# A transformer block on one Trainium2 core: normalising the next stage's first tile in the stage ahead, loops written out on two engines, and two fp32 matmuls split in two

## Chip, cores and metric

The kernel runs on one core of a Trainium2 chip. Its time is the device time of one execution, in microseconds (us). A core has four computing engines, each with a queue of its own: TensorE (PE in the profile), VectorE (DVE), ScalarE (ACT) and GpSimd (POOL). SyncE (SP) issues most DMAs. The engines run side by side and meet only at semaphores: an instruction that waits for one holds up everything behind it on its own engine.

## What is computed

A block of three residual steps over 8 sequences of 1024 tokens with 512 features, all in fp32: half a feed-forward, an attention with a delta rule, and half a feed-forward again.

```python
x = x + 0.5 * ffn(layernorm(x))
x = x + attn(layernorm(x))
x = x + 0.5 * ffn(layernorm(x))

# ffn: x_prev is x one token earlier, zero at a sequence's start
xr = mu_r * x + (1.0 - mu_r) * x_prev
xk = mu_k * x + (1.0 - mu_k) * x_prev
out = sigmoid(xr @ W_r.T) * (square(relu(xk @ W_k.T)) @ W_v.T)

# attn, first part (the stage "ain"): a causal convolution of 4 taps
q = silu(short_conv_1d(x @ Wq + bq, q_conv)); k, v likewise; q, k then divided by their norms per head
alpha, beta, gate = sigmoid(x @ Wa + ba), sigmoid(x @ Wb + bb), silu(x @ Wg + bg)
```

## The kernel before

Everything is stored with features on the 128 partitions and tokens along the free axis: a tile is [128, 4, 512], that is 512 features of 512 tokens. There are NT = 16 tiles. Five stages follow one another, with a barrier of all engines between them: the first feed-forward (`ffn1`), the q/k/v stage (`ain`), the recurrence (`rec`), the attention's output (`aout`) and the second feed-forward (`ffn2`). Both feed-forwards come from `ffn_phase`, the q/k/v stage from `attn_in_phase`. Each engine's program is written by hand, and its order is the order of the calls in `slot(...)`; nothing is scheduled.

**Products.** Every large product is made of three fp32r matmuls (`product`, L46): weight and operand are each split into a high and a low part of reduced precision, and high x high, high x low and low x high are added up in PSUM. A 512x512 product of a tile is 4 groups `m` of 12 matmuls.

**Layer norm.** VectorE adds the four feature tiles to one (`sums`, L178 and L180 in `ffn_phase`), TensorE multiplies by a matrix of 1/512 (`mean`, one fp32 matmul of 512 columns), VectorE subtracts (`centre`), ScalarE squares, GpSimd adds (`squares`), TensorE takes the variance per token (`var`), then VectorE adds epsilon (L200), ScalarE takes the root, VectorE the reciprocal (L202) and lays it on diagonals (L204), and TensorE spreads it over all partitions with a matrix of ones (`spread_rstd`, one fp32 matmul). VectorE multiplies (`normalise`).

**Feed-forward slots.** In slot `t` TensorE does `mean(t + 1)`, r (4 groups), k group 0, `var(t + 1)`, k group 1, `spread_rstd(t + 1)`, k groups 2 and 3, then v. The last slot, `slot(NT - 1, False)`, has no tile ahead and leaves the three small steps out. VectorE, ScalarE, GpSimd and TensorE run these slots in loops (`Fori`) with a few written out at the ends.

**The q/k/v stage.** In slot `t` TensorE does alpha/beta (12 matmuls, `ain_ps_ab`), then twelve groups u of q, k and v with four gate groups between them; `var(t + 1)` stands behind group 3, `spread_rstd(t + 1)` and `mean(t + 2)` behind group 5 and the second gate group. ScalarE reads each group out of PSUM (`shift`), VectorE convolves it (`convolve`: two copies of 3 columns and three operations of 512), ScalarE applies silu. A slot of VectorE begins with `mask_tails` (L806), which zeroes the 3 columns carried over from the tile before where a sequence starts, and ends with `decays`. SyncE stores decay rows only after `decays` (`ends_ready`): 4 DMAs, 4 more, and then the gate tile (L687); ScalarE's next gate group waits for that store. VectorE and ScalarE run two slots in one round of a `Fori` (L891 on VectorE), six rounds, slots 1 to 12; slot 0 and slots 13 to 15 are written out.

**The start of the q/k/v stage.** SyncE loads tile 0, the weight q, alpha/beta weights, 12 tiny bias pieces, weights g, k, v, biases and taps, then tile 1. VectorE goes through sums(0), casts of q and k, centre(0), the low parts, alpha/beta weights, the norm of tile 0, sums(1), the low part of tile 0, centre(1). TensorE stands at mean(0), var(0), spread_rstd(0), mean(1) and then the first slot.

## Time and profile before

| | us |
|---|---|
| median of 3 runs | 3439.56 (3439.38 to 3450.98) |
| the profiled execution: its own time | 3438.4 |
| its span, first to last instruction | 3436.7 |
| ffn1, up to its last VectorE instruction | 602.3 |
| first instruction of ain / first alpha/beta matmul | 607.2 / 643.25 |
| first matmul of ain's last slot | 1471.2 |
| TensorE busy | 3218.8 (94%) |
| VectorE busy | 2755.4 (80%) |

Times in the trace count from the span's start. A row of a timeline is an instruction, or several alike, with its start, its duration and the engine; "[2.40 <-ACT ...]" says that the engine had been idle for 2.40 us and what ended that. A matmul's duration includes filling the array, so the distance from one start to the next is what it takes of TensorE, not its duration. An fp32 matmul shows as two rows (x2). A wait "for issue" is idle time for which the profile knows no semaphore.

### The profile page before, as it was taken

The page shows a single profiled execution, that of the slowest core. Times are in us where ns is not written, and L with a number is a line of the kernel's source. Part 1 is how long each engine was busy: PE and PEld are TensorE (multiplying, and loading weights), DVE is VectorE, ACT ScalarE, POOL GpSimd, SP SyncE. Part 2 cuts the span into 40 slices and gives each one's busy share as a digit, 9 for nine tenths or more (in the row PEclk, how much of TensorE's full clock was granted, in tenths as well). Part 3 has the DMA queues.
Part 4 walks back from the last instruction along what each step waited for, and adds up shares of the span by engine and source line. Part 5 has one row for each costly group of instructions (what it writes and reads, how often), then busy time and mean ns, then how long its engine had stood idle before and what let it go on. Part 6 is the DMA issues. An engine that isn't in the chain of part 4 may idle for free. (4 is left out here: it accounts for less than half of the span.)

```text
span 3436.7 us, 190745 instructions
## 1 busy us (share of the span) xinstructions
PE 3218.8 (94%) x83236; PEld 2722.1 (79%) x83236; DVE 2755.4 (80%) x4776; ACT 1516.0 (44%) x2285; POOL 1300.2 (38%) x1195
## 2 busy tenths in 40 slices
PE   7999999699999999977999999999996988999999
PEld 5888888477777767757999999999995766888887
DVE  6776765798898989876999999999997857767765
ACT  4545454467676777751111111111113324455454
POOL 1232232200000000005788888888884421232322
PEclk9999999799999999988999999999997998999999
DMA  3112121233332323236777777777765772121221
GB/s 123 73 73 110 73 110 52 108 113 93 98 102 89 103 92 103 86 102 165 198 199 200 199 201 199 200 201 199 199 182 172 228 230 99 73 106 77 79 104 61
DMA packets 486578, 453.14 MB, mean 132 GB/s; under 512 B 55504, under 2 KB 448848, under 8 KB 467280
## 3 DMA queue, kind: packets, MB, share of 16 engines
q1 hardware_dynamic: 483632, 449.50, 43.4%
q10 hardware_dynamic: 2848, 2.56, 0.3%
q8 instruction: 35, 0.57, 0.1%
q14 instruction: 63, 0.52, 0.0%
HBM read 331.33 MB, written 120.60 MB: 132 GB/s over the span
## 5 line engine op out<-in xcount | busy, mean ns | idle before, releaser
L350 POOL TENSOR_TENSOR ffn_out<-ffn_gate,ffn_xres 128x512 f32<-128x512 f32 x128 | 171.0, 1364 | 783.6 <-DVE ffn_gate L254 783.2
L819 DVE SCALAR_TENSOR_TENSOR ain_conv<-ain_padded,ain_taps,ain_conv 128x512 f32<-128x512 f32 x576 | 447.2, 776 | 20.5
L1530 ACT ACTIVATE rec_u<-rec_ps_end 128x256 f32<-128x256 f32 x128 | 49.0, 383 | 632.2 <-PE rec_ps_end L1582 632.2
L909 POOL TENSOR_TENSOR ain_half<-ain_sq 128x1024 f32<-128x1024 f32 x16 | 44.8, 2797 | 731.9 <-ACT ain_sq L925 731.9
L1298 POOL TENSOR_TENSOR rec_d_norm<-rec_dmat,rec_early 128x512 f32<-128x512 f32 x128 | 162.7, 1271 | 176.0 <-DVE rec_dmat L1380 176.0
L46 PE MATMUL ffn_ring<-ffn_mixkh,ffn_wkh 128*128 128x512 f32 x512 | 218.2, 426 | 6.5 <-DVE ffn_mixkl L196 6.5
L46 PE MATMUL ffn_ring<-ffn_mixrh,ffn_wrh 128*128 128x512 f32 x512 | 215.2, 420 | 9.2 <-DVE ffn_mixrl L306 9.2
L46 PE MATMUL ffn_ring<-ffn_mixkh,ffn_wkl 128*128 128x512 f32 x512 | 202.8, 396 | 0.0
L46 PE MATMUL ffn_ring<-ffn_mixrh,ffn_wrl 128*128 128x512 f32 x512 | 201.7, 394 | 0.0
L46 PE MATMUL ffn_ring<-ffn_act_h,ffn_wvh 128*128 128x512 f32 x512 | 201.6, 394 | 0.0
L46 PE MATMUL ffn_ring<-ffn_mixkl,ffn_wkh 128*128 128x512 f32 x512 | 201.1, 393 | 0.0
L46 PE MATMUL ffn_ring<-ffn_act_h,ffn_wvl 128*128 128x512 f32 x512 | 200.9, 392 | 0.0
L46 PE MATMUL ffn_ring<-ffn_mixrl,ffn_wrh 128*128 128x512 f32 x512 | 200.0, 391 | 0.0
L46 PE MATMUL ffn_ring<-ffn_act_l,ffn_wvh 128*128 128x512 f32 x512 | 198.7, 388 | 0.0
L959 ACT ACTIVATE ain_buf<-ain_conv 128x512 f32<-128x512 f32 x192 | 120.9, 630 | 160.7 <-DVE ain_conv L819 159.8
L1582 PE MATMUL rec_ps_scores<-rec_qk_pe,rec_kb 32*32 32x64 f32 x8192 | 143.1, 218 | 35.8 <-POOL rec_kb L1290 29.7
L1304 POOL TENSOR_TENSOR rec_d_pair<-rec_d_norm,rec_masks 128x512 f32<-128x512 f32 x128 | 163.0, 1274 | 10.0
L1329 POOL TENSOR_TENSOR rec_gqk<-rec_qkv,rec_late 128x512 f32<-128x512 f32 x128 | 163.0, 1273 | 0.7 <-PE rec_ps_chain L1582 0.7
L200 DVE TENSOR_SCALAR ffn_var_tok<-ffn_mean 128x4 f32<-128x4 f32 x30 | 4.9, 163 | 193.8 <-PE ffn_mean L453 193.8
L1582 PE MATMUL rec_ps_chain<-rec_kwp,rec_u 32*32 32x64 f32 x8192 | 143.5, 217 | 17.4 <-issue 15.1
L374 ACT ACTIVATE ffn_mixkh<-ffn_mixk 128x2048 fp32r<-128x2048 f32 x32 | 61.4, 1919 | 213.9 <-DVE ffn_mixk L189 213.9
L1582 PEld LDWEIGHTS rec_ps_scores<-rec_qk_pe,rec_kb 32*32 32x32 f32 x8192 | 122.3, 106 | 37.5 <-issue 36.7
(247 smaller groups left out, 9888.4 us busy)
## 6 DMA issues: line engine op xcount, KB each, us to landing
rec_early<-coeffs SPq DMA_DIRECT2D x512, 128.0 KB, 3.0
streams<-ain_buf SPq DMA_DIRECT2D x48, 1024.0 KB, 5.1
rec_qkv<-streams SPq DMA_DIRECT2D x126, 384.0 KB, 3.4
rec_qk_pe<-streams SPq DMA_DIRECT2D x127, 256.0 KB, 3.3
rec_late<-coeffs SPq DMA_DIRECT2D x504, 64.0 KB, 2.3
ffn_xres<-in_x SPq DMA_DIRECT2D x16, 1024.0 KB
ain_x<-x SPq DMA_DIRECT2D x16, 1024.0 KB, 4.8
gate<-ain_gate SPq DMA_DIRECT2D x16, 1024.0 KB, 4.2
```

The source lines that it names most:

```text
L46: last = nc.tensor.matmul(out, w[:, k, m * width:(m + 1) * width], x[:, k, :], start=(k == 0 and n == 0), stop=(k == KT - 1 and n == 2))
L200: nc.vector.tensor_scalar_add(var_tok[:], ps_var[:, 0:KT], LN_EPS).then_inc(var_copied, 1)
L350: added = nc.gpsimd.tensor_tensor(out[:, m, :], gate[:, m, :], xres[:, m, :], ALU.add)
L374: nc.scalar.activation(mix_h[n][:], mix[n][:], ACT.Copy).then_inc(mix_high, 1)
L819: nc.vector.scalar_tensor_tensor(out=out[:], in0=pad[:, n:n + TOK], scalar=taps[:, u // KT, u % KT, n:n + 1], in1=out[:], op0=ALU.mult, op ...
L909: nc.gpsimd.tensor_tensor(half2[:], sq[:, 0:2, :], sq[:, 2:4, :], ALU.add).then_inc(halved2, 1)
L959: nc.scalar.activation(view, conv[u % 3][:].rearrange("p (c i) -> p c i", i=CH), ACT.Silu).then_inc(silued, 1)
L1298: nc.gpsimd.tensor_tensor(d_norm[:], dmat[:].unsqueeze(1).to_broadcast(pair), early[s][:, K_QNORM:K_KNORM + 1].rearrange("p k b g i -> p k ...
L1304: nc.gpsimd.tensor_tensor(d_pair[:], d_norm[:, 1].unsqueeze(1).to_broadcast(pair), masks[:, IN_BLOCK:OFF_BLOCK + 1, :].rearrange("p w (g i ...
L1329: nc.gpsimd.tensor_tensor(gqk[:].rearrange("p w (b g) i -> p w b (g i)", b=2), qkv[s][:, :, NQ:NK_ + 1].rearrange("p b w g i -> p w b (g i)"),
L1530: nc.scalar.activation(u[:], ps_end[:, :, 1, :], ACT.Copy).then_inc(u_ready, 1)
L1582: last = nc.tensor.matmul(out(rows, g), lhs_t(rows, g), rhs(rows, g), start=g in firsts, stop=True, skip_group_check=True)
```

## The change

1. **Tile 0 of ain is normalised in ffn1.** A buffer `normed` outlives both stages and takes the place of `xc` in both. ffn1 gets `norm_next=True`: its slot NT - 2 also loads tile 0 of its own output and sums it, and its last slot does mean, centre, squares, variance, deviation and spread for it, and then `normalise_next`. ain starts with `high(0, 0)` and `low(0, 0)`, its semaphores for the skipped steps are raised at once, and the loads and preparations are put in another order; all four high parts of the weights are ScalarE's now.
2. **VectorE's and ScalarE's ain programs are written out**, all 16 slots. `mask_tails` becomes `clear_tails`, a memset in even slots alone. TensorE, GpSimd and SyncE keep their loops.
3. **Mean and spread in both feed-forwards are split in high and low part**: two fp32r matmuls in place of one fp32 matmul each, for all means but those of tiles 0 and 1, and all spreads. ScalarE makes `sum_h`, VectorE `sum_l`; `sums(t + 2)` moves ahead of `mix_rest(t + 1, "r", 0)`. The reciprocal is split by two operations of 4 columns, and the diagonals are 1024 wide instead of 512.

```diff
@@ ffn_phase @@
+        rstd_diag = sb("rstd_diag", [P, 2, KT, P], F32R)
 ...
+            def sum_rest(t):
+                dve.wait_ge(sum_high, t - 1)
+                nc.vector.tensor_tensor(sum_l[:], sum1[:], sum_h[:].bitcast(F32), ALU.subtract).then_inc(sum_split, 1)
 ...
-                nc.vector.tensor_tensor(rstd_diag[:], ident[:].unsqueeze(1).to_broadcast([P, KT, P]),
-                                        rstd_tok[:].unsqueeze(2).to_broadcast([P, KT, P]), ALU.mult).then_inc(diagonal, 1)
+                nc.vector.tensor_copy(rstd_split[:, 0, :], rstd_tok[:]).then_inc(rstd_high, 1)
+                dve.wait_ge(rstd_high, t + 1)
+                nc.vector.tensor_tensor(rstd_split[:, 1, :], rstd_tok[:], rstd_split[:, 0, :].bitcast(F32),
+                                        ALU.subtract).then_inc(rstd_low, 1)
+                dve.wait_ge(rstd_low, t + 1)
+                nc.vector.tensor_tensor(rstd_diag[:], ident[:].unsqueeze(1).unsqueeze(1).to_broadcast([P, 2, KT, P]),
+                                        rstd_split[:].bitcast(F32).unsqueeze(3).to_broadcast([P, 2, KT, P]),
+                                        ALU.mult).then_inc(diagonal, 1)
 ...
+            def normalise_next():
+                dve.wait_ge(spread, NT + 1)
+                nc.vector.tensor_tensor(xc[:], xc[:], ps_rstd[:].unsqueeze(1).to_broadcast([P, KT, TOK]), ALU.mult)
 ...
-            slot(NT - 2, 1)
-            slot(NT - 1, 0)
+            slot(NT - 2, 2 if norm_next else 1)
+            slot(NT - 1, "norm" if norm_next else 0)
 ...
+            def sum_round(t):
+                act.wait_ge(summed, t)
+                act.wait_ge(mean_done, t)
+                nc.scalar.activation(sum_h[:], sum1[:], ACT.Copy).then_inc(sum_high, 1)
 ...
-                pe.wait_ge(summed, t)
-                nc.tensor.matmul(ps_mean[:], mean_w[:], sum1[:], start=True, stop=True).then_inc(mean_done, 1)
+                    pe.wait_ge(sum_split, t - 1)
+                    nc.tensor.matmul(ps_mean[:], mean_r[:], sum_h[:], start=True, stop=False)
+                    nc.tensor.matmul(ps_mean[:], mean_r[:], sum_l[:], start=False, stop=True).then_inc(mean_done, 1)
 ...
+                for part in range(2):
+                    last = nc.tensor.matmul(ps_rstd[:], ones_r[:], rstd_diag[:, part].rearrange("p j n -> p (j n)"),
+                                            start=(part == 0), stop=(part == 1))
 ...
@@ attn_in_phase @@
-            sp.dma_start(x[:], src[0, :, :, :]).then_inc(x_loaded, 16)
+            sp.sem_inc(x_loaded, 16)
+            sp.dma_start(wab_in[:], wab_dram).then_inc(ab_loaded, 16)
             sp.dma_start(stage["q"], w_dram["q"]).then_inc(w_loaded["q"], 16)
+            sp.wait_ge(centred, 1)
+            sp.dma_start(x[:], src[1, :, :, :]).then_inc(x_loaded, 16)
+            for n in "gkv":
+                sp.dma_start(stage[n], w_dram[n]).then_inc(w_loaded[n], 16)
 ...
-                nc.vector.tensor_tensor(tail[:].unsqueeze(1), tail[:].unsqueeze(1), start_mask[:, bass.ds(t, 1), :, :],
-                                        ALU.mult).then_inc(tails_masked, 1)
+                nc.vector.memset(tail[:], 0.0).then_inc(tails_masked, 1)
 ...
-            with dve.Fori(0, NT // 2 - 2) as r:
-                slot(2 * r + 1, 1)
-                slot(2 * r + 2, 0)
-            slot(NT - 3, 1)
+            for t in range(1, NT - 2):
+                slot(t, t % 2)
 ...
-            mean(0)
-            var(0)
-            spread_rstd(0)
+            for done in (mean_done, var_done, spread_done):
+                pe.sem_inc(done, 1)
             mean(1)
```

VectorE, late in a feed-forward slot of the loop, behind the low parts of the activation, before (`ffn_half` and `ffn_sum` are the sums of the tile after next, `mixr` and `mixk` the operands of r and k):

```order
L196 TENSOR_TENSOR ffn_mixrl<-ffn_mixr,ffn_mixrh 128x2048
L177 REGISTER_ALU
L178 TENSOR_TENSOR ffn_half<-ffn_x 128x1024
L180 TENSOR_TENSOR ffn_sum<-ffn_half 128x512
L189 SCALAR_TENSOR_TENSOR ffn_mixk<-ffn_diff,ffn_mu,ffn_xn 128x512 x4
```

The same place after the change:

```order
L189 TENSOR_TENSOR ffn_half<-ffn_x 128x1024
L191 TENSOR_TENSOR ffn_sum<-ffn_half 128x512
L210 REGISTER_ALU
L211 TENSOR_TENSOR ffn_mixrl<-ffn_mixr,ffn_mixrh 128x2048
L195 TENSOR_TENSOR ffn_sum_l<-ffn_sum,ffn_sum_h 128x512
L204 SCALAR_TENSOR_TENSOR ffn_mixk<-ffn_diff,ffn_mu,ffn_xn 128x512 x4
```

The sums moved ahead of r's low part, and one operation of 512 columns was added behind it.

VectorE at the start of ain, before, from the first operation that reads data to the second centring:

```order
L772 TENSOR_TENSOR ain_half<-ain_x 128x1024
L774 TENSOR_TENSOR ain_half<-ain_half 128x512
L722 CAST ain_wqh<-ain_buf 128x2048
L780 TENSOR_TENSOR ain_xc<-ain_x,ain_ps_mean 128x2048
L726 TENSOR_TENSOR ain_wql<-ain_buf,ain_wqh 128x2048
L722 CAST ain_wkh<-ain_buf 128x2048
...
L796 TENSOR_TENSOR ain_xc<-ain_xc,ain_ps_rstd 128x2048
L772 TENSOR_TENSOR ain_half<-ain_x 128x1024
L774 TENSOR_TENSOR ain_half<-ain_half 128x512
L801 TENSOR_TENSOR ain_xl<-ain_xc,ain_xh 128x2048
L767 TENSOR_TENSOR ain_bias_tap<-ain_bias,ain_taps 128x12
L780 TENSOR_TENSOR ain_xc<-ain_x,ain_ps_mean 128x2048
```

And after:

```order
L844 TENSOR_TENSOR ain_xl<-normed,ain_xh 128x2048
L800 COPY ain_conv<-ain_wab_in 128x16x4 x3
L804 CAST ain_wab_h<-ain_conv 128x512
L806 TENSOR_TENSOR ain_wab_l<-ain_conv,ain_wab_h 128x512
L768 TENSOR_TENSOR ain_wql<-ain_buf,ain_wqh 128x2048
L815 TENSOR_TENSOR ain_half<-ain_x 128x1024
L817 TENSOR_TENSOR ain_half<-ain_half 128x512
...
L768 TENSOR_TENSOR ain_wkl<-ain_buf,ain_wkh 128x2048
L810 TENSOR_TENSOR ain_bias_tap<-ain_bias,ain_taps 128x12
L823 TENSOR_TENSOR normed<-ain_x,ain_ps_mean 128x2048
```

The low part of tile 0 is first, the casts have left VectorE, and only one sum and one centring (of tile 1) stand ahead of slot 0.

VectorE at the end of a round of ain's loop, before (the next row is the first of the slot after the loop; inside, the branch goes back to slot 2r + 1):

```order
L830 SCALAR_TENSOR_TENSOR ain_gamma<-ain_decay,ain_alpha_beta 128x512
L832 COPY ain_gamma_end<-ain_gamma 128x16
L891 REGISTER_ALU
L891 COMPARE_AND_BRANCH
L806 TENSOR_TENSOR ain_tail<-ain_tail,ain_start_mask 128x36
L814 COPY ain_padded<-ain_tail 128x3
```

And after, between slots 0 and 1:

```order
L872 SCALAR_TENSOR_TENSOR ain_gamma<-ain_decay,ain_alpha_beta 128x512
L874 COPY ain_gamma_end<-ain_gamma 128x16
L856 COPY ain_padded<-ain_tail 128x3
L858 COPY ain_tail<-ain_padded 128x3
```

The branch is gone, and in odd slots nothing stands between the decays and the first convolution.

## Rows read from the trace of the kernel before

**Rows 1.** The page's costliest groups: ScalarE's copy of a whole tile to fp32r.
```profile
L374 ACT ACTIVATE ffn_mixkh<-ffn_mixk 128x2048 fp32r<-128x2048 f32 x32 | 61.4, 1919 | 213.9 <-DVE ffn_mixk L189 213.9
```

**Rows 2.** Busy time by stretch: span; PE, PEld, DVE, ACT, POOL; clock; DMA.
```profile
0.00:601.60 601.60, 581.79 (x2506) 465.40 (x2506) 413.81 (x458) 294.62 (x361) 157.97 (x99) 0.99 0.23 88
601.60:643.20 41.60, 8.05 (x14) 3.28 (x14) 31.86 (x39) 8.91 (x6) 17.05 (x8) 0.54 0.45 173
643.20:1471.20 828.00, 801.55 (x3478) 605.02 (x3478) 734.86 (x1131) 596.19 (x850) 62.27 (x30) 0.99 0.31 95
```

**Rows 3.** Timeline of TensorE: a mean in ffn1 and the matmuls behind it.
```profile
176.66 1.02 PE L447 MATMUL ffn_mean<-ffn_sum,ffn_mean_w 128*128 128x512 f32 x2
...
177.75 0.39 PE L46 MATMUL ffn_ring<-ffn_mixrl,ffn_wrh 128*128 128x512 f32 x1
177.97 0.39 PE L46 MATMUL ffn_ring<-ffn_mixrh,ffn_wrl 128*128 128x512 f32 x1
```

**Rows 4.** Waits in 40 to 602 us: TensorE's largest (total, times, longest).
```profile
PE ffn_ring L46 <- DVE ffn_mixkl L196: 3.3, 1, 3.3
```

**Rows 5.** Timelines of VectorE and TensorE in the same slot of ffn1.
```profile
157.28 0.69 DVE L204 TENSOR_TENSOR ffn_rstd_diag<-ffn_ident,ffn_rstd_tok 128x512 f32<-128x512 f32 x1
...
171.06 2.29 DVE L196 TENSOR_TENSOR ffn_mixrl<-ffn_mixr,ffn_mixrh 128x2048 fp32r<-128x2048 f32 x1 [0.86 <-ACT ffn_mixrh L374]
...
174.52 0.69 DVE L180 TENSOR_TENSOR ffn_sum<-ffn_half 128x512 f32<-128x512 f32 x1
...
159.31 1.02 PE L459 MATMUL ffn_rstd<-ffn_rstd_diag,ffn_ones 128*128 128x512 f32 x2
```

**Rows 6.** Timelines of SyncE, VectorE and TensorE at ain's start.
```profile
607.21 0.34 SPq L645 DMA_DIRECT2D ain_x<-x  x1
...
612.52 1.22 DVE L772 TENSOR_TENSOR ain_half<-ain_x 128x1024 f32<-128x1024 f32 x1 [2.61 <-DMA ain_x<-x]
...
641.05 2.08 PE L1055 MATMUL ain_ps_mean<-ain_half,ain_mean_w 128*128 128x512 f32 x2 [6.32 <-DVE ain_half L774]
643.25 0.79 PE L46 MATMUL ain_ps_ab<-ain_xh,ain_wab_h 128*128 128x512 f32 x1
```

**Rows 7.** DMA issues: count, KB each, median us from issue to landing.
```profile
ain_buf<-in_wq SPq DMA_DIRECT2D x1, 1024.0 KB, 7.0
...
ain_buf<-in_wv SPq DMA_DIRECT2D x1, 1024.0 KB, 10.1
```

**Rows 8.** Waits in 660 to 1500 us, within ain: total, times, longest.
```profile
ACT ain_gate L974 <- DMA gate<-ain_gate: 37.1, 10, 5.7
...
PE ain_ps_rstd L1067 <- DVE ain_rstd_diag L791: 26.3, 10, 4.0
DVE ain_tail L806 <- issue: 24.5, 6, 4.9
...
DVE ain_rstd_tok L789 <- ACT ain_std_tok L929: 21.3, 10, 2.4
```

**Rows 9.** Timeline of VectorE: the first instruction of ain's slots 2, 3, 4, 12, 13 and 14.
```profile
759.89 0.20 DVE L806 TENSOR_TENSOR ain_tail<-ain_tail,ain_start_mask 128x36 f32<-128x36 f32 x1
...
819.06 0.20 DVE L806 TENSOR_TENSOR ain_tail<-ain_tail,ain_start_mask 128x36 f32<-128x36 f32 x1 [4.79 <-issue]
...
870.97 0.20 DVE L806 TENSOR_TENSOR ain_tail<-ain_tail,ain_start_mask 128x36 f32<-128x36 f32 x1
...
1319.02 0.20 DVE L806 TENSOR_TENSOR ain_tail<-ain_tail,ain_start_mask 128x36 f32<-128x36 f32 x1
...
1374.63 0.20 DVE L806 TENSOR_TENSOR ain_tail<-ain_tail,ain_start_mask 128x36 f32<-128x36 f32 x1
...
1428.84 0.19 DVE L806 TENSOR_TENSOR ain_tail<-ain_tail,ain_start_mask 128x36 f32<-128x36 f32 x1
```

**Rows 10.** Timelines of SyncE and VectorE in ain's slot 2.
```profile
764.11 0.36 SPq L687 DMA_DIRECT2D gate<-ain_gate  x1
...
775.22 0.18 DVE L789 RECIPROCAL ain_rstd_tok<-ain_std_tok 128x4 f32<-128x4 f32 x1 [2.40 <-ACT ain_std_tok L929]
```

More of the change, by code:

```diff
@@ L244, in slot @@
                 act_rest(t, 3)
+                if ahead == 2:
+                    sums(t + 2)
                 if ahead:
@@ L341, in squares, with slot @@
                 nc.gpsimd.tensor_tensor(sum2[:], half2[:, 0, :], half2[:, 1, :], ALU.add).then_inc(summed2, 1)
-            def slot(t, more):
+            def slot(t, more, last=False):
                 if more:
@@ L352, in slot @@
                         added.then_inc(out_ready, 1)
-                    elif not more:
+                    elif last:
                         added.then_inc(out_piece, 1)
@@ L358, in _ @@
                 slot(t, True)
-            slot(NT - 1, False)
+            slot(NT - 1, norm_next, last=True)
         @block.scalar
@@ L438, in _ @@
             high(0, "k", 1)
-            with act.Fori(0, NT - 1) as t:
-                slot(t, True)
-            slot(NT - 1, False)
+            with act.Fori(0, NT - 2) as t:
+                slot(t, 2)
+            slot(NT - 2, 2 if norm_next else 1)
+            slot(NT - 1, "norm" if norm_next else 0)
         @block.tensor
@@ L651, in _ @@
                     at, head = m * HD + r * HG, r // 2 * H + m * HG
[L652 to L656 removed]
+                    sp.dma_start(ab_bias[at:at + HG, :], ab_bias_dram[head:head + HG, :]).then_inc(ab_bias_loaded, 16)
             def load_x(t):
@@ L706, in _ @@
         def _(dve):
+            for done in (halved, summed, centred, var_copied, inverted, diagonal, norm_step):
+                dve.sem_inc(done, 1)
             nc.vector.memset(ab_bias[:], 0.0).then_inc(padded_w, 1)
@@ L1042, in _ @@
             slot(0, 0, first=True)
-            with act.Fori(0, NT // 2 - 2) as r:
-                slot(2 * r + 1, 1)
-                slot(2 * r + 2, 0)
-            slot(NT - 3, 1)
+            for t in range(1, NT - 2):
+                slot(t, t % 2)
             slot(NT - 2, 0, ahead=1)
```

113 lines of the change are left out of this document (58 added, 55 removed).

## The prediction

> **What bounds the kernel.** I read the page's totals first (they are in the table above): TensorE is busy 94% of the span, VectorE 80%. Such shares average over stages, so the stretches come next [rows 2]. In ffn1 (0 to 601.6) TensorE is busy 581.79 of 601.60 us; between ffn1's last matmuls and ain's first alpha/beta matmul it is busy 8.05 of 41.60 us at a granted clock of 0.54; in ain up to its last slot 801.55 of 828.00. So there are three places to cost: TensorE's own work in the two feed-forwards, the start of ain, and the 26 us that TensorE idles within ain. The waits name who holds it there: in the steady part of ffn1 its largest wait is one of 3.3 us [rows 4], so it is bound by its own instructions; in ain it waits 26.3 us in 10 places for the diagonals of VectorE [rows 8].
>
> **Part 3, the split mean and spread: -23.0 us.** The mean starts at 176.66 and the second matmul behind it at 177.75; one matmul steps by 0.229 us here (177.75 to 177.97, and over a whole product the same), so the fp32 matmul takes 177.75 - 176.66 - 0.23 = 0.86 us of TensorE [rows 3]. Two fp32r matmuls of the same 512 columns take 0.46. Each mean and each spread gives 0.40 us back, as TensorE has no other wait in these slots [rows 4]. Per stage the means of tiles 2 to 15 (14) and the spreads of tiles 1 to 15 (15) count: 29 x 0.397 = 11.5 us, twice 23.0. The first spread, at half the clock, gains about what VectorE's longer chain costs ahead of it, and I set it at nothing (within 0.5 either way).
>
> The cover must hold. VectorE's diagonals start at 157.28 and take 0.69, so they end at 157.97, and TensorE comes to the spread at 159.31 [rows 5]: 1.34 us to spare. Added are two operations of 4 columns, which step by about 0.20 each (the 36-column one takes 0.20, rows 9), and 512 more columns of diagonals: 1.22 for 1024 columns [rows 6] against 0.69. That is 0.93 us, and 0.4 us is left. For the mean: the sum ends at 175.21 and TensorE wants it at 176.66 [rows 5]. The sums (1.22 + 0.69) now run ahead of r's low part, where VectorE idled 0.86 us for ScalarE, so about 1.0 us is really added ahead of that low part; it ends at 174.4 instead of 173.35, the added subtraction at 175.1. ScalarE's rounding of the sum (0.63 us) falls under the 2.29 of r's low part. TensorE wants the mean at 176.3 then: covered by 1.1 us. The k mixes start when they did. If a cover fails, each microsecond of it costs 31 us over the spreads.
>
> **Part 1a, added to ffn1's last slot: +1.9 us.** Mean and spread, 2 x 0.46, and the variance, which a slot's sum gives: the period of 35.62 us less 144 x 0.229 less 2 x 0.86 is 0.93. VectorE, ScalarE and GpSimd do what they do in every other slot. The load of tile 0 in slot 14 is one like the others; SyncE's wait for the first store has long been met. Nothing else is added behind the last matmul.
>
> **Part 1b, the start of ain: -21.9 us.** Call the stage's first instruction S (607.21 before, rows 6). Before, alpha/beta starts at 643.25 = S + 36.0. After: q is issued 0.4 us behind S; tile 0 took from its issue at 607.21 to VectorE's start at 612.52, 5.3 us [rows 6], so q lands at S + 5.7. ScalarE's cast of 2048 columns takes 1.92 [rows 1], to 7.6; VectorE's low part 2.29 (the same shape as in rows 5), to 9.9. Tile 1 is issued right behind q; q, issued 0.4 us behind tile 0, took 7.0 us [rows 7], so landed 2.1 us after it, and tile 1 is there at about S + 8. Its sums (1.22 + 0.69) follow q's low part, to 11.9. mean(1) stands ahead of slot 0 on TensorE: it took 643.25 - 641.05 = 2.2 us at the low clock [rows 6], to S + 14.1. The low part of tile 0 (1.92 + 2.29 from S + 0.5) is done at 4.7 and alpha/beta's weights at about 6.5, both earlier. 36.0 - 14.1 = 21.9.
>
> What is late next: k's and v's weights. v is the fifth megabyte; at 2.1 to 2.6 us each it lands near S + 15.6, with ScalarE's cast at 17.5; bias, taps, centre(1) (2.3) and the row choice (1.7) put VectorE's slot 0 near S + 21.6, and the first convolution waits for ScalarE's square and shift, to about S + 23.2, where it was S + 44. That is 9.1 us behind alpha/beta instead of 8, and VectorE idled 2.3 us for the variance in slot 0, so 1.1 us of lag is covered. Bounds: if the megabytes land together instead of in turn, tile 1 comes at S + 15.5 (five of them from S + 0.4), and 16.4 us is won; more than 22.5 is hardly possible, since q's path alone needs 9.9 + 1.9 + 2.2.
>
> **Part 2, the loop written out: -15 us.** VectorE waits 24.5 us "for issue" at the head of a slot, practically all in five waits of 4.8 to 4.9 us, at the branch back to every second slot [rows 8, 9]. Straight code does not show them: slots 0 and 13 to 15, written out already, have none. But they are not worth 24.5. Slot 2 takes from 759.89 to the end of its decays at 814.27 (819.06 - 4.79), 54.4 us; slot 3, behind a stall, takes 51.9, to 870.97 [rows 9]. The missing 2.4 is in the rows of slot 2: the reciprocal waits 2.40 us for ScalarE's root [rows 10]. ScalarE is late because its gate group waits for the gate's store (37.1 us in 10 waits, rows 8), and this store is issued 4.2 us after VectorE's decays end (759.86 to 764.11), behind 8 small DMAs [rows 10]. That chain runs from the end of one VectorE slot into the next, so during the stall at the branch it runs on, and the wait is gone there. Take the stall away and the wait of 2.4 comes back: 54.3 per slot for all. From slot 2's start to slot 14's are 1428.84 - 759.89 = 668.95 us for 12 slots; 12 x 54.3 = 651.6, that is 17.3 less. The mask of 0.33 a slot is before the same wait and is worth nothing. Slots 12 and 13, which follow no stall, took 55.6 and 54.2 (1319.02, 1374.63, 1428.84, rows 9), 54.9 on average; by that it is 10.1. I take 15, nearer the row that repeats. TensorE needs 52.6 us a tile where it doesn't wait, so it will still idle about 1.6 us for each spread.
>
> The Trainium skill (Runtime: NRT & Kernel Launch, section "Instruction fetch mechanics") says that a taken branch whose target lies outside a small window of pages stalls for a fetch, and that straight code is fetched ahead. The trace agrees that there is a stall (4.8 to 4.9 us); what it is worth is the trace's to say, and taken alone the rule leads to the first rival.
>
> **Sum.** Against the profiled execution's 3438.4: 3438.4 - 23.0 + 1.9 - 21.9 - 15 = 3380.4. The median of the runs lies 1.2 above it: 3381.5.
>
> **Rivals.**
> - *The stalls are worth their full length.* If VectorE's slots stay at 51.9 because ScalarE's lateness came from the stall's aftermath in TensorE and not from the store, 24.5 comes back and the masks' 2.6 (13 x 0.20): 3369.5. For it: TensorE's waits of 3.7 to 4.0 us for the diagonals follow the stalls. Against: slots 12 and 13 have the same 2.4 us wait without a stall. 13%.
> - *Loads land together at ain's start*, price 5.5: 3387. Against: before, the weights landed 2.5 us apart though issued 0.4 apart. 10%.
> - *The diagonals come late.* If 1024 columns with the doubled broadcast, written in fp32r, take two cycles each, the chain grows by 2.1 instead of 0.93, 0.8 us past its cover, 31 times: 3406. Against: all fp32r writes of VectorE here run at the fp32 rate (2.29 for 2048, rows 5). 9%.
> - *The change leaves the start as it is*: TensorE waits at mean(1) for something behind k's weights, 12 us later than worked out: 3394. The order of VectorE speaks against it. 3%.
> - *The other side: written-out code stalls on its own.* If each slot of fresh code cost VectorE two exposed fetches of 4.85, 13 slots would pay 126 us and the sum is 3507, slower. It decides at 12% less than one exposed stall a slot (58/63). Slots 0 and 13 to 15 speak against it. 3%; and 2% for one stall a slot or the like, about no change.
>
> **How the numbers follow.** The forecast case has 60%, the rivals 38%, 2% the rest between. The range reaches from the first rival, with 2.5 for its unknowns, to the case of loads landing together with the low bound of part 2 (3387 + 5): 3367 to 3394. The diagonals' case and the other side stay out, 14%. Faster by over 0.5% (17 us, about what a measurement of this kernel can tell from none) in all but the last: 95%; within 2%; slower 3%.
>
> **What would show it.** Feed-forward: slots of 34.8 us for 35.6, no wait of TensorE for the diagonals or the split sum. ain's start: alpha/beta 14 us behind the stage's first instruction, mean(1) just ahead, released by VectorE's sum. ain: no wait for issue on VectorE, the reciprocal's wait of 2.4 to 2.7 in every slot from 3 on, slots of 54.3. Everything from rec on keeps its length but for ffn2's 11.5 us. It would be wrong if slots fell below 53.5 or TensorE's waits for spreads went away.

## The result, and the profile after

The changed kernel takes **3394.92 us** (median of 4 runs, 3392.48 to 3397.35); the kernel before, run beside it, 3440.09. The ratio is 0.9863, with a 95% interval of 0.9849 to 0.9878: 45 us less by the medians, 47 by the ratio. Run again in another set it gave 0.9868 (0.9851 to 0.9884). The forecast was 3381.5, with a range of 3367 to 3394. The median is 0.9 us above that range's end; the ratio, applied to the 3439.56 that the forecast started from, gives 3392.4, just inside. Some 45 to 47 us came where 58 were expected. The profiled execution took 3392.5 us with a span of 3390.5, 46.2 less than before's 3436.7.

The same three stretches as in [rows 2], with the same columns (start and end; span; TensorE, its weight load, VectorE, ScalarE, GpSimd; granted clock; DMA share; GB/s):

```profile
0.00:593.97 593.97, 572.61 (x2518) 467.95 (x2518) 446.11 (x515) 307.84 (x379) 158.26 (x101) 0.99 0.24 91
593.97:612.32 18.35, 1.09 (x3) 0.57 (x3) 10.22 (x25) 5.73 (x3) 2.56 (x5) 0.61 0.73 287
612.32:1436.70 824.38, 799.89 (x3480) 603.26 (x3478) 742.82 (x1125) 598.56 (x852) 72.15 (x32) 0.99 0.32 96
```

ffn1 is 7.6 us shorter and the gap between the stages 23.3 (41.60 to 18.35), but ain from its first alpha/beta matmul to that of its last slot only 3.6 (828.00 to 824.38), where 15 were forecast. Most of the difference is in that line.

**The feed-forwards.** TensorE's timeline, the mean and the product behind it, to be read against [rows 3], and the mean one slot later:

```profile
176.20 0.39 PE L492 MATMUL ffn_mean<-ffn_sum_h,ffn_mean_r 128*128 128x512 f32 x1
176.43 0.40 PE L493 MATMUL ffn_mean<-ffn_sum_l,ffn_mean_r 128*128 128x512 f32 x1
176.66 0.39 PE L46 MATMUL ffn_ring<-ffn_mixrh,ffn_wrh 128*128 128x512 f32 x1
...
211.00 0.39 PE L492 MATMUL ffn_mean<-ffn_sum_h,ffn_mean_r 128*128 128x512 f32 x1
```

The mean is two steps of 0.23 us, 0.46 in all (176.20 to 176.66), and the slot 34.80 us instead of 35.61. VectorE's chain to the diagonals and the sum's low part, against [rows 5]:

```profile
157.23 0.17 DVE L219 CAST ffn_rstd_split<-ffn_rstd_tok 128x4 fp32r<-128x4 f32 x1
157.43 0.16 DVE L221 TENSOR_TENSOR ffn_rstd_split<-ffn_rstd_tok,ffn_rstd_split 128x4 fp32r<-128x4 f32 x1
157.63 1.22 DVE L224 TENSOR_TENSOR ffn_rstd_diag<-ffn_ident,ffn_rstd_split 128x1024 fp32r<-128x1024 f32 x1
...
173.73 0.69 DVE L195 TENSOR_TENSOR ffn_sum_l<-ffn_sum,ffn_sum_h 128x512 fp32r<-128x512 f32 x1
```

The 1024 columns take 1.22 us as costed, and the sum's low part is there at 174.42, 1.8 us before TensorE asks for it at 176.20. TensorE waits in no steady slot for either.

**The start of ain.** Timelines of VectorE and TensorE, against [rows 6]:

```profile
609.23 1.22 DVE L815 TENSOR_TENSOR ain_half<-ain_x 128x1024 f32<-128x1024 f32 x1
...
611.23 2.07 PE L1088 MATMUL ain_ps_mean<-ain_half,ain_mean_w 128*128 128x512 f32 x2 [17.26 <-DVE ain_half L817]
612.32 1.41 PE L46 MATMUL ain_ps_ab<-ain_xh,ain_wab_h 128*128 128x512 f32 x1
```

The stage's first instruction is at S = 599.68; mean(1) begins when VectorE's sum is done, and alpha/beta starts at S + 12.6, where it was S + 36.0: 23.4 us won, 21.9 forecast. But behind that start VectorE and GpSimd look like this:

```profile
614.65 4.30 DVE L768 TENSOR_TENSOR ain_wkl<-ain_buf,ain_wkh 128x2048 fp32r<-128x2048 f32 x1 [3.13 <-ACT ain_wkh L1062]
618.88 4.59 DVE L810 TENSOR_TENSOR ain_bias_tap<-ain_bias,ain_taps 128x12 f32<-128x12 f32 x1
...
629.05 1.14 DVE L856 COPY ain_padded<-ain_tail 128x3 f32<-128x3 f32 x1 [1.62 <-ACT ain_conv L982]
...
612.22 4.59 POOL L938 TENSOR_TENSOR ain_wgl<-ain_gate,ain_wgh 128x2048 fp32r<-128x2048 f32 x1 [11.89 <-ACT ain_wgh L1062]
617.26 6.18 POOL L938 TENSOR_TENSOR ain_wvl<-ain_buf,ain_wvh 128x2048 fp32r<-128x2048 f32 x1 [0.45 <-ACT ain_wvh L1062]
...
644.39 1.13 PE L1100 MATMUL ain_ps_rstd<-ain_rstd_diag,ain_ones 128*128 128x512 f32 x2 [3.05 <-DVE ain_rstd_diag L834]
```

A product of 12 columns takes 4.59 us. It ends when GpSimd's low part of v ends (623.4). k's low part, 2.29 us of work, ends 2.1 us behind GpSimd's low part of g (616.8), and GpSimd's own low part of v, 4.6 us of work, takes 6.2. The first convolution starts at S + 29.4 instead of S + 23.2, and TensorE waits 3.05 us for the spread's diagonals. From alpha/beta to the end of slot 0's decays it is 66.6 us (612.32 to 678.96); before, 60.3 (643.25 to 703.59). So 6.3 of the 23.4 us are given back.

**The slots of ain.** The last instruction of the decays in slots 0, 1, 2, 3, 4, 5 and 14 on VectorE, and from slot 3 the gate's store of the slot before on SyncE, the reciprocal on VectorE and the gate on ScalarE (against [rows 9, 10]):

```profile
678.78 0.18 DVE L874 COPY ain_gamma_end<-ain_gamma 128x16 f32<-128x16 f32 x1
734.98 0.17 DVE L874 COPY ain_gamma_end<-ain_gamma 128x16 f32<-128x16 f32 x1
789.26 0.18 DVE L874 COPY ain_gamma_end<-ain_gamma 128x16 f32<-128x16 f32 x1
843.61 0.18 DVE L874 COPY ain_gamma_end<-ain_gamma 128x16 f32<-128x16 f32 x1
898.23 0.17 DVE L874 COPY ain_gamma_end<-ain_gamma 128x16 f32<-128x16 f32 x1
953.28 0.18 DVE L874 COPY ain_gamma_end<-ain_gamma 128x16 f32<-128x16 f32 x1
...
1443.62 0.18 DVE L874 COPY ain_gamma_end<-ain_gamma 128x16 f32<-128x16 f32 x1
...
793.72 0.36 SPq L736 DMA_DIRECT2D gate<-ain_gate  x1
...
804.77 0.18 DVE L832 RECIPROCAL ain_rstd_tok<-ain_std_tok 128x4 f32<-128x4 f32 x1 [2.40 <-ACT ain_std_tok L963]
...
797.66 0.69 ACT L1008 ACTIVATE ain_gate<-ain_ps_ring,ain_bias 128x512 f32<-128x512 f32 x1 [4.25 <-DMA gate<-ain_gate]
```

The slots 2 and 3 take 54.3 us as forecast, slot 4 takes 54.6, and the slots 5 to 12 take 55.1 to 55.7. Slots 1 to 14 together: 764.8 us here; before (703.41 to 1478.16) 774.8. The waits in 660 to 1470 us (total, times, longest), against [rows 8]: no wait "for issue" at a slot's head is left, and the reciprocal waits 2.40 us in 13 slots instead of 8 (slot 1 has a shorter wait in both).

```profile
ACT ain_gate L1008 <- DMA gate<-ain_gate: 63.1, 15, 5.4
...
PE ain_ps_rstd L1100 <- DVE ain_rstd_diag L834: 20.6, 12, 2.9
...
DVE ain_rstd_tok L832 <- ACT ain_std_tok L963: 32.4, 14, 2.4
```

### The profile page after: what moved, and what is told of

The parts are those of the page before. It is cut to its first block and busy times, and to the rows that moved or that the text cites. A ratio compares the mean times of both kernels' runs of the same rounds, so it can differ in the third digit from the quotient of the medians.

```text
span 3390.5 us, 189736 instructions
## 1 busy us (share of the span) xinstructions
PE 3186.6 (94%) x83236; PEld 2718.0 (80%) x83236; DVE 2794.9 (82%) x4862; ACT 1537.9 (45%) x2316; POOL 1296.8 (38%) x1195
## 5 line engine op out<-in xcount | busy, mean ns | idle before, releaser
L46 PE MATMUL ffn_ring<-ffn_mixrh,ffn_wrh 128*128 128x512 f32 x512 | 202.0, 395 | 10.9 <-DVE ffn_mixrl L337 10.9
L46 PE MATMUL ffn_ring<-ffn_mixkh,ffn_wkh 128*128 128x512 f32 x512 | 205.8, 402 | 6.5 <-DVE ffn_mixkl L211 6.5
L1361 POOL TENSOR_TENSOR rec_gqk<-rec_qkv,rec_late 128x512 f32<-128x512 f32 x128 | 163.3, 1276 | 0.7 <-PE rec_ps_chain L1614 0.7
L370 POOL TENSOR_TENSOR ffn_half<-ffn_diff 128x1024 f32<-128x1024 f32 x31 | 111.9, 3611 | 109.4 <-ACT ffn_diff L396 109.4
L1614 PEld LDWEIGHTS rec_ps_scores<-rec_qk_pe,rec_kb 32*32 32x32 f32 x8192 | 122.1, 106 | 37.4 <-issue 36.6
```

The costliest lines, as they stand in the source:

```text
L46: last = nc.tensor.matmul(out, w[:, k, m * width:(m + 1) * width], x[:, k, :], start=(k == 0 and n == 0), stop=(k == KT - 1 and n == 2))
L370: nc.gpsimd.tensor_tensor(half2[:], diff[:, 0:2, :], diff[:, 2:4, :], ALU.add).then_inc(halved2, 1)
L1361: nc.gpsimd.tensor_tensor(gqk[:].rearrange("p w (b g) i -> p w b (g i)", b=2), qkv[s][:, :, NQ:NK_ + 1].rearrange("p b w g i -> p w b (g i)"),
L1614: last = nc.tensor.matmul(out(rows, g), lhs_t(rows, g), rhs(rows, g), start=g in firsts, stop=True, skip_group_check=True)
```

## The experiments

Each kernel was timed beside the kernel before. "14 slots" is the time from the end of the decays in ain's slot 0 to that in slot 14; "stalls" are VectorE's waits for issue at the head of a slot, their total and count in 660 to 1470 us; the sixth of each six is the way into the loop (0.2 to 0.6 us), the other five are the branches back.

| kernel | median, us | ratio (95%) | stalls, us | 14 slots, us |
|---|---|---|---|---|
| before | 3438.0 to 3443.2 in the four sets | 1 | 24.5, 6 | 774.8 |
| the change | 3394.9 | 0.9863 (0.9849 to 0.9878) | none | 764.8 |
| the change again | 3392.6 | 0.9868 (0.9851 to 0.9884) | none | 764.9 |
| no low parts on GpSimd | 3388.8 | 0.9856 (0.9841 to 0.9871) | none | 766.4 |
| other order at ain's start | 3394.6 | 0.9871 (0.9856 to 0.9886) | none | 766.8 |
| split alone, on before | 3431.4 | 0.9967 (0.9955 to 0.9979) | 36.6, 6 | 785.9 |
| loops alone, on before | 3430.9 | 0.9964 (0.9951 to 0.9978) | none | 765.7 |
| the change, loops back | 3393.5 | 0.9863 (0.9848 to 0.9878) | 2.5, 6 | 765.4 |
| before, loop 24 further on | 3431.1 | 0.9972 (0.9961 to 0.9983) | 2.5, 6 | 765.5 |
| before, loop 12 further on | 3450.2 | 1.0029 (1.0017 to 1.0040) | 36.2, 6 | 785.3 |
| gate first, on before | 3431.6 | 0.9983 (0.9974 to 0.9992) | 28.3, 6 | 764.1 |
| gate first, on the change | 3361.7 | 0.9782 (0.9769 to 0.9796) | none | 734.8 |
| before, 24 further on and gate first | 3401.1 | 0.9885 (0.9870 to 0.9900) | 2.5, 6 | 734.8 |
| gate first and other order, on the change | 3357.4 | 0.9754 (0.9741 to 0.9767) | none | 734.1 |

The slots repeat to 0.1 us between the two profiles of the change. The whole does not: the recurrence and the output projection, whose code is the same in all of these, took 1276 to 1295 us together from profile to profile. A difference of a few us is therefore read in the stage that the edit touches.

### The start of ain: what lengthened VectorE's work

The first kernel is the change with GpSimd's two low parts left out; it writes zeros in their place:

```diff
             def weight_low(n):
                 pool.wait_ge(w_high[n], 1)
-                nc.gpsimd.tensor_tensor(W[n][1][:], stage[n], W[n][0][:].bitcast(F32), ALU.subtract).then_inc(w_split[n], 1)
+                nc.gpsimd.memset(W[n][1][:].bitcast(F32), 0.0).then_inc(w_split[n], 1)
```

> The changed kernel, with GpSimd's low parts of g's and v's weights left out: it writes zeros in their place, so the products of g and v lack their low weights' share; every wait stands. Theory (mutual blocking): VectorE's low part of k falls from 4.30 to 2.28 us, bias_tap from 4.59 to 0.17 us; slot 0 starts near S+21.6 as forecast and ab to the end of slot 0's decays goes from 66.6 to near 60 to 61 us; 5 to 6.5 us less than the changed kernel. Rival 1 (the arrival of k's weights and of the taps held them): the two keep starts and ends, 0 us. Rival 2 (the DMA traffic slows VectorE): durations stay long, 0 us.

```profile
612.97 2.29 DVE L768 TENSOR_TENSOR ain_wkl<-ain_buf,ain_wkh 128x2048 fp32r<-128x2048 f32 x1 [2.93 <-ACT ain_wkh L1062]
615.18 0.17 DVE L810 TENSOR_TENSOR ain_bias_tap<-ain_bias,ain_taps 128x12 f32<-128x12 f32 x1
...
610.53 1.80 POOL L938 MEMSET ain_wgl<- 128x2048 f32 x1 [11.79 <-ACT ain_wgh L1062]
615.52 1.82 POOL L938 MEMSET ain_wvl<- 128x2048 f32 x1 [3.18 <-ACT ain_wvh L1062]
```

The timelines of VectorE and GpSimd: with S = 598.09 here, k's low part takes 2.29 and bias_tap 0.17 us, although the weights and taps come over the same queue at the same time. GpSimd's two memsets end before k's low part and start behind bias_tap, so nothing of GpSimd's runs beside either. TensorE has no wait left in slot 0, and alpha/beta to the end of the decays is 61.5 us (610.83 to 672.28) instead of 66.6. Both rivals, the arrival of the data and slow VectorE under DMA traffic, fall. The median is 6 us lower, but the ratio only 0.0007 (2 us), and the two intervals overlap: the whole cannot tell this from none, the 5.2 us in the slot can.

The Trainium skill (SBUF — State Buffer, section "SBUF: two separate sides") says that VectorE and GpSimd share a pair of SBUF ports as an exclusive lock: of a GpSimd operation and a VectorE one in a two-port mode, or a GpSimd operation that reads SBUF and a VectorE one with two SBUF inputs, whichever starts second is blocked until the first has ended. The trace of the change agrees, in both directions: the 12-column product waited 4.4 us, and GpSimd's low part 1.6. So semaphores are not the only place where two engines meet, whatever the section on the chip says. The trace of before already showed this: VectorE's three copies of 64 columns, 0.39 us in the change, took 5.30 there while GpSimd worked on squares and on the low part of g.

```profile
624.87 5.30 DVE L757 COPY ain_conv<-ain_wab_in 128x64 f32<-128x64 f32 x3
```

The second edit keeps the work and moves it. Bias and taps are loaded ahead of tile 1 on SyncE, and on VectorE:

```diff
-            weight_low("k")
             bias_taps()
             centre(1)
             choose_rows()
+            weight_low("k")
```

> The changed kernel with another order at the start of the q/k/v stage: the loads of the bias and the taps ahead of the tile and the weights of g, k and v, and VectorE's order sums(1), select_heads, bias_taps, centre(1), choose_rows, weight_low(k). In the changed kernel as it stands VectorE reached slot 0 27.6 us after the stage's first instruction, since k's low part (4.30 us) and the tiny bias_tap (4.59 us) each ended with a low part on GpSimd. Theory (GpSimd's low parts of g and v, 4.6 and 6.2 us, and VectorE's elementwise work with both operands in SBUF keep each other out): bias_tap falls to 0.17 us and centre(1) begins near S+14, k's low part ends with or right after GpSimd's low part of v (S+24), slot 0 starts near S+24 to S+25 instead of S+27.6, the wait for the spread's diagonal goes from 3.05 us to under 1: 2 to 5 us less, 3390 to 3393. Rival (VectorE waited for the arrival of weights, bias and taps, not for the other engine): the early loads alone bring slot 0 to near S+21, 6 us less, and no operation of VectorE is longer than in other places.

VectorE's timeline of this kernel:

```profile
611.73 0.18 DVE L810 TENSOR_TENSOR ain_bias_tap<-ain_bias,ain_taps 128x12 f32<-128x12 f32 x1
613.59 2.29 DVE L823 TENSOR_TENSOR normed<-ain_x,ain_ps_mean 128x2048 f32<-128x2048 f32 x1 [1.68 <-PE ain_ps_mean L1088]
615.79 2.02 DVE L783 TENSOR_TENSOR ain_decay<-ain_ident 128x16 f32<-128x16 f32 x1
...
618.05 7.06 DVE L789 TENSOR_TENSOR ain_decay<-ain_decay 128x4 f32<-128x4 f32 x3
```

centre(1), with one operand in PSUM, runs in 2.29 us beside GpSimd's low part of g. But the row choice now met it: three additions of at most 4 columns took 7.06 us, held first by the low part of v and then by GpSimd's sums. Slot 0 is 64.7 us, 2.0 less than in the change. The first convolution starts no sooner than in the change (S + 29.5; S + 24 to 25 was expected for the slot), and by the ratio (0.9871) this kernel is no faster: the 2 to 5 us expected did not come. The blocking moved to the smallest operations, and I had not costed them. The version that works puts the row choice ahead of centre(1), where VectorE waits for the mean anyway; it is the last kernel below.

### Which part brought what

The first kernel is the kernel before with part 3 alone, the second with part 2 alone (its expectation says every fourth tile for the clearing of the tails; it is every second), the third is the change with the loops and the mask put back:

```diff
-            for t in range(1, NT - 2):
-                slot(t, t % 2)
+            with dve.Fori(0, NT // 2 - 2) as r:
+                slot(2 * r + 1, 1)
+                slot(2 * r + 2, 0)
+            slot(NT - 3, 1)
```

> The kernel before with the split mean and spread alone, in both feed-forward stages; its q/k/v stage as it was, with its tile 0 normalised there. Theory: 29 steady slots at 34.80 instead of 35.61 us, first slots 0.8 to 1 us later at the ring's start, ffn2's first slot 1 to 3.5 us shorter where TensorE no longer waits before var: 20 to 25 us less than before, 3413 to 3420. The changed kernel against this one then carries the first normalisation moved and the loops written out, 20 to 25 us. Rival (part of what both feed-forward stages gained in the changed kernel came from the moved normalisation or is noise between runs): under 18 us.

> The kernel before with VectorE's and ScalarE's q/k/v programs written out and the tails cleared every fourth tile, and nothing else. Theory (a stall is worth what it exceeds the gate's chain by): slots 2 to 12 near 55.0 us, the 14 from 1 on 10 us less than before: 3427 to 3430. Rival (a stall is worth its whole 4.85 us): 29 us less, 3409.

> The changed kernel with the loops and the mask of the tails put back in the q/k/v stage. Theory: the alternation of slots near 59 and 52.6 us is back, the stage 9 to 11 us longer than the changed kernel: 3404 to 3406. Rival (the start and the loops interact, since VectorE enters the loop 20 us sooner against TensorE): more than 4 us away from that.

The split alone gave 12 us instead of 20 to 25. Its feed-forwards are 10.1 and 10.4 us shorter, near the 11.5 costed for each, but its q/k/v stage, whose code nobody touched, is 11 us longer: VectorE's stalls at the branch went from 4.9 us to between 7.1 and 7.4. The number is the rival's (under 18 us), its reason is not. The loops alone gave 12 us, 9 of them in the 14 slots, where 10 were expected. Putting them back into the change cost nothing, against 9 to 11 expected, so that expectation and the mechanism behind it (the stalls come back with the loop) were wrong: the stalls are 0.5 us there. The waits of VectorE for issue, of the split alone and of the change with loops back:

```profile
DVE ain_tail L854 <- issue: 36.6, 6, 7.4
```

```profile
DVE ain_tail L854 <- issue: 2.5, 6, 0.5
```

So the loop's own code does not fix the stall. Counted in the assembled programs, the branch to the loop of VectorE is 289 instructions behind its head in all of them; the head is number 328 in the kernel before, 340 with the split alone and 348 with loops back. Two more kernels shift it: the kernel before with its one memset of the tails, ahead of the loop, cut into 25 pieces or 13 pieces:

```diff
-            nc.vector.memset(tail[:], 0.0)
+            cells = tail[:].rearrange("p u n -> p (u n)")
+            for n in range(24):
+                nc.vector.memset(cells[:, n:n + 1], 0.0)
+            nc.vector.memset(cells[:, 24:3 * 3 * KT], 0.0)
```

> The kernel before, with its one memset of the tails cut into 25, so that VectorE's q/k/v loop lies 24 instructions further on in its program (its first instruction is number 328 before, 352 here; 340 with the split alone, whose stalls were 7.1 to 7.4 us, and 348 in the changed kernel with loops back, whose were 0.5). Theory (the stall at the loop's start depends only on where the loop lies against the blocks in which code is fetched, with a block's edge between 340 and 348): stalls of 0.5 us, slots 2 to 12 near 55.0, the stage some 9 us shorter: 3428 to 3434. Rival (what removed the stalls with loops back was the normalisation moved away, or other traffic): stalls of 4.8 us, within 2 us of before (3438 to 3443).

> The same with 13 memsets: the loop begins at 340, as with the split alone. Theory (place of the loop): stalls of 7.1 to 7.4 us as there, the stage 9 to 11 us longer than before: 3447 to 3454. Rival (the split's other effects lengthened the stalls): stalls of 4.8 us, no difference.

```profile
816.86 0.20 DVE L809 TENSOR_TENSOR ain_tail<-ain_tail,ain_start_mask 128x36 f32<-128x36 f32 x1 [0.52 <-issue]
```

```profile
822.81 0.20 DVE L809 TENSOR_TENSOR ain_tail<-ain_tail,ain_start_mask 128x36 f32<-128x36 f32 x1 [7.02 <-issue]
```

The head of slot 3 in VectorE's timeline: 0.52 us with the loop 24 further on, 7.02 with it 12 further on. The kernel is 9.6 us faster by the one and 10 us slower by the other, from memsets of one column. With all else as before, moving the loop changes the stall as forecast, and both rivals fall. The place is not quite all: with the gate's store first, below, the loop is at 328 and its stalls run from 4.8 to 6.6 us, which no run explains. ScalarE keeps its loop in these two kernels, and with 24 further on the 14 slots take 765.5 us, where both engines written out took 765.7: writing out ScalarE's is worth nothing. The Trainium skill (Runtime: NRT & Kernel Launch, section "Instruction fetch mechanics") gives blocks of 256 instructions, of which an engine holds two. 289 instructions fit in two blocks or lie over three: the runs agree if an edge lies between 340 and 348. That edge is inferred from the lengths of the stall, no row shows it, and why 340 costs more than 328 is open.

### What a stall is worth, and what covers it

```diff
                 store_stream(t, NV)
+                sp.wait_ge(gate_ready, KT * t + 2 * KT)
+                sp.dma_start(gate_dram[bass.ds(t, 1), :, :, :].rearrange("a p k n -> (a p) k n"), gate[:]).then_inc(gate_stored, 16)
                 sp.wait_ge(ends_ready, t + 1)
```

The gate's store leaves from behind the eight small DMAs of the decays and goes ahead of them; nothing else changes.

> The kernel before with the same move on SyncE. There VectorE stalls 4.85 us once in every second slot with nothing awaited, and each stall was forecast to be worth only 2.4 us, since the gate's chain ran on beside it. Theory: the chain's wait goes (2.40 us in the slots without a stall, none in those with one, which already had none), VectorE needs 51.9 in an undisturbed slot and 56.8 in one with a stall, TensorE 52.6: the mean slot 54.7 instead of 55.5, 8 to 12 us less over 12 slots, 3428 to 3432. Rival (the stall is worth its whole 4.85 us and the chain nothing): no difference, within 2 us.

> The changed kernel with one move on SyncE: in each slot of the q/k/v stage the gate's store is issued ahead of the decays' eight small DMAs instead of behind them. Theory (VectorE's wait of 2.40 us for its reciprocal in each slot comes from the chain decays' end, eight small issues, gate store, ScalarE's gate, ScalarE's root): the store begins some 4 us sooner, ScalarE's wait for it goes, the 2.40 us too, VectorE has more slack, TensorE no longer waits 0.6 to 2.9 us a slot for the diagonals and runs at 52.6 to 53 us a slot instead of 55: 13 slots by 2.0 to 2.4, 25 to 30 us less than the changed kernel, 3365 to 3370. Rival (ScalarE's own order sets its root: its wait moves to the convolution or to the sums of the ring): under 8 us.

> The kernel before with the loop moved on by 24 instructions and the gate's store issued first. Alone, the second gave 6 us, and the first is expected to give 9. Theory (stall and gate chain cover one another, so that each is worth little while the other stands): every slot from 2 on at 52.6 us, the 14 slots 735 us instead of 775: 36 to 40 us less, 3400 to 3405. Rival (they add): 15 us less, 3425.

On the kernel before, the move gave 6 us in the median, less than the 8 to 12 expected, and 10.6 in the 14 slots (the last slot takes 1.4 more; the rest lies in stages whose code is unchanged). Shifting the loop gave 9.6. Together they give 39.6 us (0.9885), not 15. On the change the move gives about 30 us, all of it in the 14 slots (764.8 to 734.8): TensorE's period is 52.59 us in every slot from 1 to 13, and it waits for no spread. SyncE, VectorE and ScalarE at the end of slot 2 and in slot 3 of the change with gate first, where slot 2's decays end at 786.26:

```profile
784.74 1.05 SPq L732 DMA_DIRECT2D gate<-ain_gate  x1
...
799.82 0.18 DVE L832 RECIPROCAL ain_rstd_tok<-ain_std_tok 128x4 f32<-128x4 f32 x1 [1.05 <-ACT ain_std_tok L963]
...
791.81 0.69 ACT L1008 ACTIVATE ain_gate<-ain_ps_ring,ain_bias 128x512 f32<-128x512 f32 x1 [1.57 <-DMA gate<-ain_gate]
```

The store begins 1.5 us ahead of the decays' end instead of 4.3 behind it, and ScalarE waits 1.57 instead of 4.25.

This is the forecast's mechanism, with its price now measured. With the gate's chain in place, a pair of slots (3 and 4, up to 11 and 12) takes on average 110.1 to 110.3 us without stalls or with stalls of 0.5, 112.1 with one of 4.9, and 114.2 to 114.3 with one of 7.0 to 7.4: the stalls cost 1.9 and 4.1, their length less about 3.0. With the chain gone, a pair takes 105.2 without a stall. On the kernel before with gate first it takes 110.5 to 111.9, 111.1 on average, with waits for issue of 5.5 to 6.6 us in it (4.8 to 6.6 at the head, and in two slots another 1.0 at a convolution): at 5.9 us they cost about their length. In the 14 slots the move alone gives 10.6 us, the shift alone 9.3, both 40.0: each of the two waits hid most of the other.

### The best version

Gate first, and at the start of ain the early loads of bias and taps with VectorE's order sums(1), select_heads, bias_taps, choose_rows, centre(1), weight_low("k"):

> Gate store first and another order at the start: bias and taps loaded ahead of x(1), VectorE's order sums(1), select_heads, bias_taps, choose_rows, centre(1), weight_low(k). Theory (mutual blocking of GpSimd's low parts and VectorE's work with two operands in SBUF): bias_tap and the row choice run before GpSimd's first low part begins (near S+13.5) at 0.17 us each, centre(1), which reads one operand from PSUM, runs beside it at 2.3 us, only k's low part meets it; the slot 0 starts near S+21 instead of S+27.6, the wait for the diagonal in slot 0 goes below 1 us: 3 to 6 us less than gate store first alone (3361.7): 3356 to 3359. Rival (the blocking only moves on into slot 0's convolutions, against GpSimd's low part of v): within 1.5 us of 3361.7.

VectorE's and TensorE's timelines:

```profile
612.21 0.55 DVE L789 TENSOR_TENSOR ain_decay<-ain_decay 128x4 f32<-128x4 f32 x3
...
622.11 2.71 DVE L856 COPY ain_padded<-ain_tail 128x3 f32<-128x3 f32 x1 [1.76 <-ACT ain_conv L982]
624.85 2.33 DVE L858 COPY ain_tail<-ain_padded 128x3 f32<-128x3 f32 x1
...
641.38 1.13 PE L1100 MATMUL ain_ps_rstd<-ain_rstd_diag,ain_ones 128*128 128x512 f32 x2 [0.28 <-DVE ain_rstd_diag L834]
```

The row choice takes its 0.55 us, TensorE's wait in slot 0 goes from 3.05 to 0.28, and the slot is 62.6 us. The blocking is not gone: k's low part (4.31 us) meets GpSimd's low part of g, and the first convolution's two copies of 3 columns, 0.17 us elsewhere, take 2.71 and 2.33 us beside GpSimd's low part of v and its sum. They have one input in SBUF each, so an operation need not have two to be held. 3357.4 us, ratio 0.9754 (0.9741 to 0.9767), is the fastest kernel of the study, 35 to 38 us below the change.

## Why the prediction was right, and where it was not

The three places were the right ones and the mechanisms of most terms held, but the saving was 46.2 us in the profiled pair, not 58. The 12 us between are, term by term: 2 more in ffn1's first slot, 5 at ain's start (1.5 won, 6.3 lost), 5 in ain's slots, 1 in unchanged stages, and 1.5 the other way in ffn2. Nearly all of them went the same way, so it is the width of the range, not the sum, that took them in.

**Part 3, -23.0: right.** The 14 slots of a feed-forward are 0.81 us shorter each, 11.3, where 11.5 was forecast, and both covers held. Set at nothing was the first spread: VectorE's longer chain starts the first product 0.8 us later (24.54 to 25.36). From there to the mean of tile 2, slot 0 takes 46.4 us instead of 45.3; but that stretch takes 44.9 to 48.1 in the other profiles, whatever the kernel, so the 1.2 is not the change's for certain. ffn2 as a whole is 13.1 shorter: 11.4 in its 14 slots, 3.2 in its first slot, which wanders in the same way, less 1.5 for a later first product. What the split alone lacks in its median is the stall that it lengthened.

**Part 1a, +1.9: right.** ffn1 is 7.6 us shorter: 11.4 less 2.0 for the first product and slot 0 leaves 1.8 added in the last slot.

**Part 1b, -21.9: right for alpha/beta (-23.4), wrong behind it.** The prediction held more than 22.5 to be hardly possible; that it was 23.4 comes in the main from a row read wrongly. The 2.2 us from the mean to alpha/beta were not the mean's: before, alpha/beta's weight load waited for the low part of tile 0,

```profile
643.25 0.29 PEld L46 LDWEIGHTS ain_ps_ab<-ain_xh,ain_wab_h 128*128 128x128 f32 x1 [1.70 <-DVE ain_xl L801]
```

and after the change, with that part long done, the step is 1.09 (611.23 to 612.32).

The step that failed is "what is late next": it lined up VectorE's work (k's low part, bias, taps, centre(1) 2.3, row choice 1.7) at the durations of single operations, and put slot 0 at S + 21.6. It came at S + 27.7, since the earlier start lays VectorE's work beside GpSimd's low parts. Before, both of GpSimd's low parts were over (at 639.2) when alpha/beta started. Cost: 6.3 us, and 5.2 of it is gone where GpSimd's low parts are.

**Part 2, -15: the mechanism right, the size below its low value of 10.1.** The 14 slots give 9.9. The stall's worth was reckoned as its length less the 2.4 us wait behind it, and all slots at 54.3; it is its length less about 3.0, and only slots 2 and 3 are 54.3. The term that was mis-sized is the gate's chain: the prediction read in slot 1 that the gate's store is issued 4.2 us behind the decays' end, and took that for all slots. It is 4.2 to 4.6 us in the slots 0 to 3, 12 and 13 of the change, but 5.0 to 5.3 in the slots 4 to 11, and the slot behind each of those takes 55.1 to 55.7. These eight slots are the ones that SyncE runs in its own loop, which the change keeps: there two register instructions, a step of some 0.07 us each, stand ahead of every DMA to form its address; slots 0 to 3 do not have them. The store behind slot 4 on SyncE, and then ScalarE and VectorE in slot 5, to be read against the rows of slot 3 above:

```profile
903.42 0.36 SPq L736 DMA_DIRECT2D gate<-ain_gate  x1
...
907.35 0.69 ACT L1008 ACTIVATE ain_gate<-ain_ps_ring,ain_bias 128x512 f32<-128x512 f32 x1 [4.97 <-DMA gate<-ain_gate]
...
909.32 0.17 DVE L856 COPY ain_padded<-ain_tail 128x3 f32<-128x3 f32 x1 [1.06 <-ACT ain_conv L982]
```

The decays of slot 4 end at 898.40, so the store comes 5.0 us behind them. ScalarE's gate waits 4.97 us for it, the convolution's square behind that gate is late, and VectorE, which does not wait there in slot 2, waits 1.06; the 2.40 for the reciprocal follows. The kernel before has the same step in the same slots (4.2 to 4.4 us in its slots 0 to 3, 5.0 to 5.3 in 4 to 11). With the gate's store ahead of the small DMAs, this wait is gone in the slots 2 to 13 and they take 52.6 on average. No run writes SyncE's loop out; worked out from these rows, that would give 0.8 us in each of eight slots, an estimate.

The clock is a rival for the 0.8 us. Behind the wait of 2.19 us that TensorE has in slot 5 the spread takes 1.87 us (0.97 in slot 4, at 860.34), and the granted clock just behind is 0.56, near the lower of its two levels (1.2 of 2.4 GHz):

```profile
915.40 2.08 PE L1100 MATMUL ain_ps_rstd<-ain_rstd_diag,ain_ones 128*128 128x512 f32 x2 [2.19 <-DVE ain_rstd_diag L834]
...
917.00:919.00 2.00, 2.00 (x4) 0.80 (x3) 1.89 (x5) 1.97 (x3) 0.00 (x0) 0.56 0.00 0
```

But the wait at 909.32 comes first: up to 915.3 the clock is 1.00. And in the kernel with the other order at ain's start slot 5 has the same 1.06 us and the same 55.1, while its spread, behind a wait of 2.24, takes 0.96 and the clock stays at 1.00:

```profile
913.79 1.12 PE L1100 MATMUL ain_ps_rstd<-ain_rstd_diag,ain_ones 128*128 128x512 f32 x2 [2.24 <-DVE ain_rstd_diag L834]
```

The forecast had the right row for the size, slots 12 and 13 at 54.9 on average, and preferred the other "that repeats".

**The rivals.** Full length of the stalls (3369.5) is wrong for the change and right without the gate's chain. Loads together (3387) has a number nearer the result than the forecast's but not its reason: q's low part was done and tile 1 there by S + 9.6. That is luck, and the range's upper end came from this rival. The diagonals' and the k weights' case did not occur, nor the other side: written-out code shows no wait for issue. Two small sums of the prediction are off and change nothing: 58 of 63 is 8% less than one exposed stall a slot, not 12%, and before, the first convolution stood at S + 44.7, 8.6 behind alpha/beta.

**What the prediction did not consider** is that the stall's length is not fixed. The change adds instructions ahead of VectorE's loop (parts 1 and 3), and those alone would have moved the stall from 4.9 to 0.5 us: with its other two parts in place, writing the loops out is worth nothing (0.9863 both ways). A price for that part holds only against the kernel before, where it measured 12 (9 in the 14 slots).

## What to carry to other kernels

When two waits end at the same place, neither is worth its length: find the chain that runs on during the stall, and price the pair, since here two edits worth 6 and 10 us were worth 40 together. When work is moved earlier on VectorE, look at what GpSimd then does beside it, down to operations of three columns. And a stall for issue at a loop's head should be looked for again after every edit ahead of the loop, and may be removed by moving the loop instead of writing it out. A chain's length read in one slot should be read in a slot of each engine's loop as well.
